# Attention with a gated FFN on one core: inverse row sums by on-chip transfers, contexts in two PSUM banks

## The reference

```python
xn = _layernorm(x)                                   # eps 1e-5
q, k = _rope(split_heads(xn @ Wq.T)), _rope(split_heads(xn @ Wk.T))   # 16 heads of 32
v = split_heads(xn @ Wv.T)
scores = einsum('bhqd,bhkd->bhqk', q, k) / sqrt(32)  # causal: -inf above the diagonal
s = merge(softmax(scores) @ v) @ Wo.T
h = gelu(bitlinear(xn, w_fc)); f = bitlinear(h, w_proj)   # ternary weights, layer norm before each
out = x + s * silu(f)
```

## Time and profile before

| | us |
|---|---|
| median of 3 runs | 1162.41 (1162.39 to 1164.09) |
| the profiled execution's own time | 1162.8 |
| its span, first to last instruction | 1161.0 |
| TensorE matmul busy | 1122.5 (97%) |
| VectorE busy | 847.5 (73%) |
| ScalarE busy | 792.0 (68%) |
| POOL busy | 525.7 (45%) |

### The profile page before, as it was taken

The page is one execution under the profiler, slowest core; times in us unless marked ns, Lnnn a source line. Parts: engine busy times, 40 slices in busy tenths (PEclk is TensorE's granted clock), DMA queues, the critical chain, the costliest instruction groups (busy, mean ns, idle before and its releaser), DMA issues.

```text
span 1161.0 us, 20071 instructions
## 1 busy us (share of the span) xinstructions
PE 1122.5 (97%) x7580; PEld 615.0 (53%) x7580; DVE 847.5 (73%) x1450; ACT 792.0 (68%) x1508; POOL 525.7 (45%) x917
## 2 busy tenths in 40 slices
PE   4989999999999999999999999999999999999997
PEld 3555644448444574446644475445844467444763
DVE  6997867798458885588756885579845888558854
ACT  4787975589735868279673796448882696827964
POOL 2135352472625635275442745257262663527434
PEclk9999999999999999999999999999999999999999
DMA  8491011730109101361016411082011910144111
GB/s 307 155 110 38 1 30 37 98 87 18 30 13 151 38 3 28 47 118 37 3 28 79 85 38 30 1 108 83 11 30 24 139 38 3 28 59 70 37 40 37
DMA packets 52586, 67.31 MB, mean 58 GB/s; under 512 B 9352, under 2 KB 34312, under 8 KB 51976
## 3 DMA queue, kind: packets, MB, share of 16 engines
q1 hardware_dynamic: 52488, 66.02, 29.8%
HBM read 31.98 MB, written 8.40 MB: 35 GB/s over the span
## 4 chain that ended last, share of the span: by engine, by line
PE 84%; ACT 7%; DVE 4%; DMA 2%; issue 1%; SPq 1%; DVEq 0%; ACTq 0%
PE banks L410 21%; PE banks L535 17%; PE banks L566 13%; PE banks L514 5%; PE banks L663 5%; PE banks L632 5%; PE banks L427 5%; PE banks L575 4%; ACT arena L863 4%; PE banks L521 2%; ACT banks L840 1%; PE banks L441 1%; ACT split_buf L786 1%; DMA stacks<-split_buf 1%; PE banks L448 1%
## 5 line engine op out<-in xcount | busy, mean ns | idle before, releaser
L840 ACT ACTIVATE banks<-banks,mix,scl 128x512 f32<-128x512 f32 (+2 forms) x384 | 248.6, 658 | 7.2 <-POOL mix L1314 4.4
L1096 DVE TENSOR_REDUCE mix<-banks 128x1 f32<-128x384 f32 (+3 forms) x352 | 217.2, 637 | 31.0 <-PE banks L521 20.1
L535 PE MATMUL banks<-xT,fcT 128*128 128x512 f16 x1024 | 228.1, 379 | 4.6 <-ACT xh_buf L809 4.4
L566 PE MATMUL banks<-proj_ones,arena 128*128 128x256 f16 (+1 forms) x1536 | 213.3, 273 | 0.0
L863 ACT ACTIVATE arena<-banks,scl 128x1280 f32<-128x1280 f32 x128 | 164.8, 1328 | 70.5 <-PE banks L632 66.9
L1300 POOL TENSOR_TENSOR split_buf<-xr_buf,split_buf 128x512 f16<-128x512 f32 x64 | 74.0, 1177 | 254.3 <-ACT split_buf L786 254.3
L1309 POOL TENSOR_TENSOR xh_buf<-xh_buf 128x512 f32<-128x512 f32 x120 | 152.4, 1270 | 48.2 <-ACT xh_buf L809 39.9
L410 PE MATMUL banks<-xT,qkT 128*128 128x512 f16 x768 | 168.7, 379 | 0.0
L535 PEld LDWEIGHTS banks<-xT,fcT 128*128 128x128 f16 x1024 | 98.5, 98 | 124.2 <-ACT xh_buf L809 9.8
L566 PEld LDWEIGHTS banks<-proj_ones,arena 128*128 128x128 f16 x1536 | 142.6, 97 | 33.8
L1314 POOL TENSOR_SCALAR mix<-mix,scl 128x1 f32<-128x1 f32 (+1 forms) x288 | 76.1, 265 | 165.6 <-DVE mix L1096 165.6
(11 more groups left out here) (156 smaller groups left out, 1507.4 us busy)
## 6 DMA issues: line engine op xcount, KB each, us to landing
stacks<-split_buf SPq DMA_DIRECT2D x192, 128.0 KB, 5.1
out_dram<-arena SPq DMA_DIRECT2D x32, 256.0 KB, 2.0
xr_buf<-in_L_attn_x_dram SPq DMA_DIRECT2D x7, 1024.0 KB, 7.3
resid<-in_L_attn_x_dram SPq DMA_DIRECT2D x28, 256.0 KB, 5.2
stacks<-in_L_ffn_w_fc_dram SPq DMA_DIRECT2D x1, 4096.0 KB, 26.8
arena<-in_L_ffn_w_proj_dram SPq DMA_DIRECT2D x1, 4096.0 KB, 14.6
mix<-norm_row SPq DMA_DIRECT2D x8, 256.0 KB, 4.8
xr_buf<-in_L_attn_x_dram SPq DMA_DIRECT2D x4, 256.0 KB, 3.8
```

The costliest lines, as they stand in the source:

```text
L535: mm = pe.matmul(banks[:, UP_BANKS[f % NUB], :], fcT[:, c, f * P:(f + 1) * P], xT[:, part, c, :], start=(c == 0 and part == 0), stop=(c == ...
L566: mm = pe.matmul(banks[:, DOWN_BANKS[h % 3], 0:cols.stop - cols.start], hid[:, part, f, t * P:(t + 1) * P], proj_ones[:, f, cols], start=( ...
L840: mm = nc.scalar.activation(block, block, ACT.Exp, scale=col(EXP_SCALE), bias=exp_bias[:, i, h0 + k:h0 + k + 1], accum_out=row_sum[:, i, h ...
L1096: nc.vector.tensor_reduce(row_max[:, i, h0:h0 + n], scores_of(r), AX_X, ALU.max).then_inc(max_ready, 1)
```

## The change

- The split of the inverses in three parts, the `selector` matrix with its set-up on POOL, and the four spreading products go. The reciprocals are transposed as float32 (16 rows), and `invT` is a float32 buffer of 16 partitions in `resid`.
- SP issues four transfers per sequence from SBUF to SBUF. Each reads four rows of `invT` and writes each of them to 32 partitions of `inv_spread`, which has two halves in turn. The first two wait for `invT`, the others for the context multiply that frees their half. The norm row's load stands between the second and third. The residual loads now wait until all four have landed.
- Groups are weighed in banks 7 and 6 in turn. A weighing waits for the multiply of two groups before, and the first also for the last centring.
- VectorE's `finish_context` waits for the transfer instead of copying bank 7, and for groups 0 to 2 it makes the cast to the high part itself. ScalarE keeps only group 3's.

```diff
-        inv_spread = split_f[:, 1024:1536]
-        invT = split_f[0:SPLITS * H, 1536:1536 + S // 2].bitcast(F16)
+        inv_spread = split_f[:, 1024:2048].rearrange("p (a t) -> p a t", a=2)
+        invT = resid[0:H, 0, :]
...
             def body(b, first=False, last=False):
                 if not first:
+                    for s in inv_dma:
+                        sp.wait_ge(s, b * 32)
                     load_resid(b - 1, 0)
...
                 if not last:
                     store_norms(b + 1)
-                    spread_norms(b + 1)
+                for g in range(NG):
+                    if g == 0:
+                        sp.wait_ge(invT_ready, b + 1)
+                    if g >= 2:
+                        sp.wait_ge(ctx_ready, b * NG + g - 1)
+                    sp.dma_start(inv_spread[:, g % 2, :], invT[GH * g:GH * (g + 1), :].unsqueeze(1).broadcast_to([GH, DK, S])
+                                 ).then_inc(inv_dma[g % 2], 16)
+                    if g == 1 and not last:
+                        spread_norms(b + 1)
...
-                    pe.wait_ge(inv_split, b + 1)
+                    pe.wait_ge(inv_ready, b + 1)
                     pe.wait_ge(centred, b * NT + 1)
                     for i in range(NT):
-                        mm = pe.transpose(banks16[0:SPLITS * H, 6, i * P:(i + 1) * P],
-                                          inv_parts[:, i].rearrange("p s h -> p (s h)"), ident16[:])
+                        mm = pe.transpose(banks[0:H, 6, i * P:(i + 1) * P], row_sum[:, i, :], ident32[:])
...
                     if j == 0:
                         if g == 0:
+                            pe.wait_ge(centred, b * NT + NT)
+                        if g == 1:
                             pe.wait_ge(invT_ready, b + 1)
-                        else:
-                            pe.wait_ge(ctx_ready, b * NG + g)
-                    if j == 1:
-                        if g == 0:
-                            pe.wait_ge(centred, b * NT + NT)
-                        pe.matmul(banks[:, 7, :], selector[:, GH * g:GH * (g + 1), :].rearrange("p h d -> p (h d)"), invT,
-                                  start=True, stop=True).then_inc(spread_ps, 1)
+                        if g >= 2:
+                            pe.wait_ge(ctx_ready, b * NG + g - 1)
...
-                        mm = pe.matmul(banks[k * DK:(k + 1) * DK, 6, j * P:S], v_sb[:, j, head * DK:(head + 1) * DK],
+                        mm = pe.matmul(banks[k * DK:(k + 1) * DK, 7 - g % 2, j * P:S], v_sb[:, j, head * DK:(head + 1) * DK],
...
-                    if h % GH == 0 and g >= 2:
-                        split_context(g - 2)
                 if not last:
                     split_tokens(b + 1)
-                split_context(2)
...
-                dve.wait_ge(inv_ready, b + 1)
-                split_parts(inv_parts, row_sum[:], INV_GROW, inv_step, b * 3, inv_split)
...
-                nc.vector.tensor_copy(invT, banks16[0:SPLITS * H, 6, 0:S]).then_inc(invT_ready, 1)
+                nc.vector.tensor_copy(invT, banks[0:H, 6, :]).then_inc(invT_ready, 1)
...
-                    dve.wait_ge(spread_ps, b * NG + g + 1)
-                    nc.vector.tensor_copy(inv_spread, banks[:, 7, :]).then_inc(spread_kept, 1)
-                    dve.wait_ge(spread_kept, b * NG + g + 1)
+                    dve.wait_ge(inv_dma[g % 2], b * 32 + 16 * (g // 2) + 16)
                     dve.wait_ge(pv_ps, b * NG + g + 1)
-                    nc.vector.tensor_tensor(ctx_f32[:, g % 2, :], banks[:, 6, :], inv_spread, ALU.mult).then_inc(ctx_ready, 1)
+                    nc.vector.tensor_tensor(ctx_f32[:, g % 2, :], banks[:, 7 - g % 2, :], inv_spread[:, g % 2, :], ALU.mult).then_inc(ctx_ready, 1)
+                    if g < NG - 1:
+                        dve.wait_ge(ctx_ready, b * NG + g + 1)
+                        nc.vector.tensor_copy(ctxT[:, 0, g, :], ctx_f32[:, g % 2, :]).then_inc(ctx_hi, 1)
```

More of the change, by code:

```diff
@@ L27 @@
 KM = KS + SPLITS
-INV_GROW = 4096.0
 ROPE_SHRINK = 1.0 / 16
@@ L129, in program @@
         row_sum = mix[:, 0, 352:416].rearrange("p (i h) -> p i h", i=NT)
-        inv_parts = mix[:, 0, 416:512].bitcast(F16).rearrange("p (i s h) -> p i s h", i=NT, s=SPLITS)
         bn = mix[:, 0, 288:288 + 6 * NT].rearrange("p (t k) -> p t k", t=NT)
@@ L149, in program @@
         mask_q = sb("mask_q", [P, P], BF16)
-        selector = sb("selector", [SPLITS * H, H, DK], F16)
         ones32 = sb("ones32", [P, 1], F32)
@@ L210, in program @@
         exp_bias_dve, exp_bias_ready, sum_ready = sem("exp_bias_dve"), sem("exp_bias_ready"), sem("sum_ready")
-        max_step, max_split, inv_ready, inv_step, inv_split = sem("max_step"), sem("max_split"), sem("inv_ready"), sem("inv_step"), sem("inv_split")
+        max_step, max_split, inv_ready = sem("max_step"), sem("max_split"), sem("inv_ready")
+        inv_dma = [sem("inv_dma0"), sem("inv_dma1")]
         invT_ps, invT_ready = sem("invT_ps"), sem("invT_ready")
-        selector_step = sem("selector_step")
         maxT_ps, maxT_ready = sem("maxT_ps"), sem("maxT_ready")
@@ L218, in program @@
         st_ps, probs_ready, probs_masked, pv_ps = sem("st_ps"), sem("probs_ready"), sem("probs_masked"), sem("pv_ps")
-        spread_ps, spread_kept, ctx_ready = sem("spread_ps"), sem("spread_kept"), sem("ctx_ready")
+        ctx_ready = sem("ctx_ready")
         ctx_hi, ctx_lo = sem("ctx_hi"), sem("ctx_lo")
@@ L1231, in _ @@
                 nc.gpsimd.memset(proj_ones[:, :, edge:edge + 1], 1.0)
-            nc.gpsimd.memset(selector[:], 0.0)
             nc.gpsimd.memset(minus_half[:], -0.5).then_inc(ln_step, 1)
@@ L1236, in _ @@
                 nc.gpsimd.affine_select(ident[:], ident[:], [[-1, P]], ALU.not_equal, 1.0, base=0, channel_multiplier=1)
[L1237 to L1241, removed]
             nc.gpsimd.affine_select(mask_q[:], mask_q[:], [[-1, P]], ALU.is_ge, MASKED, base=0, channel_multiplier=1).then_inc(consts, 1)
```

## The result

The changed kernel takes **1278.3 us** (median of four runs, 1275.74 to 1278.48), the one before 1162.55 beside it: a ratio of **1.099, 95% interval 1.0976 to 1.1003**. The forecast was 1267, range 1180 to 1335. The span is 1276.4 us for 1161.0.

What follows compares the result with a forecast made beforehand. TensorE, busy 97% of the span, was taken as the bound. Seven hand-overs losing 13.1 us each (91.7) plus 12.25 in the last sequence lift the span from 1161.0 to 1264.95, time 1267 us, range 1180 to 1335.

Steps and rivals of the forecast that it cites:

- transfers at a partition's rate, on the path: SP's SBUF-to-SBUF transfers: four source partitions at 7.7 GB/s each give 30.8 GB/s, delaying TensorE 13.1 us per sequence; chance 0.70.
- D: Time one 256 KB inverse transfer moves data, between first packets and last byte; taken as 8.5 us.
- Landings: The four inverse transfers stand behind one another and land at 587.2, 595.7, 605.1 and 613.6 us.
- Value products: Next sequence's products on TensorE wait behind VectorE's third multiply and token splits, starting at 607.1 after 4.8 us idle.
- The step that failed: Third value tile waits for its bank, behind ScalarE's last context cast, until 615.6; value products end at 620.8, not 607.74.
- the clock: TensorE may fall to its lower clock in the value products after gaps: 0 to 3 us a sequence, in the range alone.
- 4D - 20.9: Loss in us per sequence from the transfers; zero at D = 5.2, a gain of 1.24 below about 4.9.
- The edits costed at little: Removing spreading products gains 1.24 us per sequence in TensorE's attention stage; casts, inverses and banks hidden or unwaited.
- Rival 1: Transfers: reading few partitions isn't limited, D = 2.7 us, all hidden, 9.9 us less, 1152.5 us; chance 0.21.
- Rival 4: Transfers hidden, but waiting for the last centring or ScalarE eats the 1.24 us: no change, 1162 us; chance 0.02.
- Rival 3: Transfers in between, D of 5.2 to 6.2 us, up to 4 us lost per sequence: 1163 to 1190 us; chance 0.03.
- Rival 2: Transfers: reading costs more than writing, D of 10.5 us and up, 21 us or more per sequence, 1335 and above; chance 0.04.

Runs made afterwards that it cites:

- experiment 4: Changed kernel plus sixteen filler products into an unused bank ahead of each later sequence's value products: 1272.51 us, ratio 1.095 to the kernel before.
- experiment 1: Changed kernel with the four source rows of each transfer 12 partitions apart instead of adjacent: 1152.9 us, ratio 0.992 to the kernel before.
- experiment 5: Changed kernel with the heads' sums reordered so each transfer's four source rows lie 4 partitions apart: 1152.71 us, ratio 0.991; repeated, 1152.8 us.
- experiment 3: Changed kernel with transfers of half the width, 1 KB packets, the multiply using that half twice: 1157.7 us, ratio 0.996 to the kernel before.
- experiment 6: Changed kernel with source rows 32 partitions apart, read from the residual tile instead of the inverses: 1163.29 us, one run.

## Why the prediction was right, and where its terms were off

**Right: transfers at a partition's rate, on the path.** TensorE's stage, which ended 31.8 us after the inverses' copy (607.74 less 575.91), ends 46.7 after it in the repetition shown. The profile of before didn't have the operation; its nearest row, on-chip copying into 16 partitions, gave 30.8 GB/s, and the runs say 25 to 27. **D, the mis-sized term,** was 256 KB at 25 to 27 GB/s, hence 9.7 to 10.5 us, and not 8.5. The rate is a block's and not a partition's: one row in each of four blocks moves 88 GB/s or more, where 7.7 GB/s a partition allowed 31. So scaling by single partitions came out near by luck of where the rows lie: the 123 GB/s of the earlier trace rows went into 16 neighbouring partitions, which are four blocks, so one block would have got the same 30.8. Where a block's edges lie was not tested; the change reads rows 4g to 4g+3. The Trainium skill ("SBUF — State Buffer", Door 1) had 27.6 for partitions 0 to 3, and the trace agrees: 25 to 27, and with 16 engines 27.

**Landings.** Forecast +10.85, +19.35, +28.75, +37.25 after the copy; multiplies at +12.4, +22.8, +31.5, +36.8. The first two are later by what D was short, once and twice. The last two come 5.2 apart and not 8.5, because a transfer is not rigidly behind another: the window from 646 shows 50 GB/s at the same engine share, twice one block's rate. Two groups, two blocks, are read at once there, as if two engines were already at the next one; that two engines alone draw a block's full rate, the window from 652 shows. This gave back what D took, and group 3 landed within 0.5 us of its forecast. That is luck: with a D of 10 the prediction's own sum gives 6 us more a sequence, 1315 us in all, and only the overlap that it left out brings it back.

**Value products.** Their start was forecast at +30.75 and is +33.4 (the third landing, late by 2.8). The queue of VectorE was right: multiply, cast, token splits, start, with 3.97 us of idle TensorE. **The step that failed** is the one behind it: that the third value tile waits for its bank, and so for ScalarE's cast of group 3. It didn't. The clock had fallen to 0.5, so the first tile alone took twice its 2.6 us, to 658.4, and ScalarE's cast ended at 657.94: its first copy then waits 0.57 for TensorE. Even at the full clock the wait would have been next to nothing: in experiment 4 the value products take 10.52 us, 0.16 more than before. I had the clock at 0 to 3 us in the range alone and the cast in the sum; it was the other way round, and the sizes are near each other: 13.7 us forecast from the start to the end of the value products with the cast, 13.35 measured by the clock, 10.36 before.

**POOL and the weighings.** POOL's remainder waits for VectorE's cast (129.9 us in all), the masks behind it, TensorE 5.26 and 1.77 us: as forecast, and as forecast neither sets the end, since the value products wait for VectorE.

**The sum.** The copies of `invT` of the first and last sequence lie 1064.2 us apart, before 962.4: 101.8 in seven hand-overs, forecast 91.7 (14.5 each against 13.1). The first of them lost most, 16.8 us (155.9 for 139.2), the others 13.7 to 15.2. In the first a load stands in SP's queue that the prediction forgot when it moved the residual loads: that of the output weights, issued at 199 us where it was at 182, and the chain goes through it for 8.1 us. From the last copy's start to the end it was 36.7 and is 51.0: 14.3, forecast 12.25. Together 116, with the first sequence's start 0.7 earlier, 115.4. The formula 4D - 20.9 would have given 19.1 a sequence for D = 10. What is left of the miss in the repetition shown is three terms: the start of the value products (+2.6), the cast's wait that did not come (-3.3), the clock (+3.0; 1.5 to 3 over the later sequences, by value products of 12.0 to 13.5 us).

**The edits costed at little.** Spreading products, selector, splits, casts and the two banks were forecast at 1.24 us per sequence. Experiments 1 and 5 show them by themselves: 135.9 to 136.0 for 137.2. One figure on the way there was misread: 5.13 less 0.1 over four exponentials is 1.26 us each and not 1.23. Nothing came of it, since in experiment 5 the chain has no exponential between the first weighing and the value products. The cast takes 0.43 us, I took 0.5. That the residual loads move behind the transfers cost nothing, as said, but for the weights behind them in the first hand-over. The norm row's load took 2.18 us to issue (before 0.32) and 19.7 to land (before 4.8), and nobody waited.

**The rivals.** Rival 1 asked for some 50 GB/s and is the kernel of experiment 5: it forecast 1152.5, and where the rows lie apart 1152.7 is measured. Rival 4 falls with it. Rival 3 was priced too high: experiments 3 and 6 have D of 5 to 5.5, where the formula gives up to 1.1 us of loss, and take 136.6 a sequence, 0.6 less than before; transfers that overlap help them too, as far as the runs tell. Rival 2's D of 10.5 was nearly met (9.7 to 10.5 by the rate, 10.4 between the first two multiplies), its reason was not: reading the same bytes again has no price of its own where blocks differ.

So the better kernel is that of experiment 5 or 1, both 0.8 to 0.9% under the one before.

## What to carry to other kernels

Where a transfer inside the chip reads few partitions, count how many blocks of four they lie in, not how many partitions or engines they are, and don't set them 32 apart, which gave half the rate: here the same 256 KB took 10 us from one block and 3 us from four, and laying four rows 4 apart cost nothing but the order of some indices. Before trusting a broadcast by DMA, work out the D at which the loss is zero (here 5.2 us) and ask which side of it the rate is on. A term that is hidden behind another shows in full only when the other is gone, so test two edits both alone and together.

## What the runs showed of the hardware

- Reading 4 rows of 2 KB, 32 times each, inside the chip: 25 to 27 GB/s from one block of four partitions, 48 with rows 32 apart, 88 with rows 4 apart, 94 with rows 12 apart, at an engine share of 0.24 to 0.26 throughout. Rows of 1 KB from one block: 24 at 0.22.
- At one block, 16 engines (share 0.90) move 27 GB/s, four (0.24) 25 to 27, two (0.12) 24. The DMA share tells that engines are occupied, not that bytes move.
- Two transfers in flight from neighbouring blocks add up: 50 GB/s.
- After 5.26 us without a product TensorE ran the next eight at a granted 0.50 (1.2 GHz); after 1.77 us at 1.00; after 3.97 us the value products began at 0.51. With sixteen fillers ahead these ran at 1.00 (10.52 us for 13.35), and the fourth weighing slowed down instead (24 products in 2.62 us for 1.50), behind a gap of 2.52 us.
- An issue on SP took 2.18 us for 0.32 behind two transfers of this kind.
